# A two-layer MetaFormer on one core: four engine orders and the PSUM bank table replaced, column scans summed by GpSimd too, all stores last

## What is computed

```python
# conv block, on layer-normed x
feat = x @ in_w + in_b                      # 64 -> 3 * 64
inp, og, lam = silu(.), sigmoid(.), sigmoid(.)
inp_f = (1 - lam) (x) inp                   # 128 channels: every pair (d, e)
h_t = lam_t * h_{t-1} + inp_t               # along H and along W, forward and backward
state = fwd_h + rev_h + fwd_w + rev_w
out = layernorm(sum_d state * og) * gamma + beta
x = x + out @ out_w + out_b
# layer 0 experts: 16 of 128 hidden, top 2 of a softmax
x = x + sum_e gate[e] * ((silu(t @ w1[e]) * (t @ w2[e])) @ w3[e])
# layer 1 experts: 8 of 256 hidden, top 2
x = x + sum_e gate[e] * (gelu(t @ W1[e] + b1[e]) @ W2[e] + b2[e])
```

## Time and profile before

| | us |
|---|---|
| median of 3 runs | 237.87 (237.5 to 238.17) |
| the profiled execution, its own time | 238.65 |
| its span, first to last instruction | 236.4 |
| PE busy | 218.6 (92%) |
| DVE busy | 182.1 (77%) |
| ACT busy | 171.8 (73%) |
| POOL busy | 139.6 (59%) |
| mean granted TensorE clock | 0.993 of full |

### The profile page before, as it was taken

One profiled execution on the slowest core, in us unless ns is written; L12 is line 12 of the kernel. 1 busy time (PEld: TensorE's weight loads), 2 busy tenths in 40 slices (PEclk: granted clock), 3 DMA queues, 4 the chain that ended last, 5 costly groups with the idle time before them and its releaser, 6 DMA issues.

```text
span 236.4 us, 3790 instructions
## 1 busy us (share of the span) xinstructions
PE 218.6 (92%) x1078; PEld 139.6 (59%) x1078; DVE 182.1 (77%) x532; ACT 171.8 (73%) x407; POOL 139.6 (59%) x222
## 2 busy tenths in 40 slices
...
GB/s 104 12 185 194 176 2 3 0 6 175 209 152 6 182 174 0 10 209 146 27 223 114 0 3 0 5 135 42 0 3 177 4 1 0 3 193 11 142 82 22
DMA packets 19088, 18.51 MB, mean 78 GB/s; under 512 B 5606, under 2 KB 12924, under 8 KB 19068
## 3 DMA queue, kind: packets, MB, share of 16 engines
...
...
## 4 chain that ended last, share of the span: by engine, by line
PE 36%; DVE 28%; ACT 15%; issue 10%; POOL 9%; POOLq 0%; DVEq 0%; ACTq 0%
PE SPARE L1567 13%; PE SPARE L1427 9%; PE SPARE L1428 8%; DVE hidden L1338 5%; PE SPARE L1443 3%; ACT silu_h L1027 2%; ACT norm_e L901 2%; POOL rstd_e L754 2%; DVE SPARE L1248 2%; DVE gated L1281 2%; DVE fwd_w L1217 2%; DVE lam_rw L1227 2%; PE SPARE L1498 2%; POOL rstd_a L754 1%; DVE stats_e L1164 1%
## 5 line engine op out<-in xcount | busy, mean ns | idle before, releaser
L1427 PE MATMUL SPARE<-tok_z,up_hi 128*128 128x512 f32 x192 | 81.5, 424 | 2.6 <-DVE hidden L1338 2.1
L1428 PE MATMUL SPARE<-tok_z,up_lo 128*128 128x512 f32 x192 | 75.6, 394 | 0.0
L626 POOL TENSOR_TENSOR total<-total,weighted 128x512 f32<-128x512 f32 x39 | 50.2, 1286 | 32.0 <-DVE weighted L1362 19.6
L1567 PE MATMUL SPARE<-hidden,down 128*64 128x512 f32 x256 | 60.9, 603 | 1.1 <-DVE hidden L1338 0.8
L1027 ACT ACTIVATE silu_h<-SPARE 128x512 f32<-128x512 f32 x64 | 37.7, 599 | 22.0 <-PE SPARE L1428 19.7
L1427 PEld LDWEIGHTS SPARE<-tok_z,up_hi 128*128 128x128 f32 x192 | 36.1, 188 | 27.5 <-issue 13.0
L1338 DVE TENSOR_TENSOR hidden<-silu_h,SPARE 128x512 f32<-128x512 f32 x64 | 42.1, 678 | 9.5 <-ACT silu_h L1027 8.0
L1428 PEld LDWEIGHTS SPARE<-tok_z,up_lo 128*128 128x128 f32 x192 | 36.2, 189 | 5.8
L1567 PEld LDWEIGHTS SPARE<-hidden,down 128*64 128x64 f32 x256 | 16.1, 136 | 31.6 <-issue 25.4
L1034 ACT ACTIVATE hidden<-SPARE,expert_bias 128x512 f32<-128x512 f32 x32 | 21.9, 685 | 6.3 <-PE SPARE L1567 5.8
L1440 PE MATMUL SPARE<-ident 128*128 128x128 f32 x162 | 23.2, 302 | 3.0 <-POOL ident L726 1.9
...
## 6 DMA issues: line engine op xcount, KB each, us to landing
...
down<-in_L_ffn_w_dram SPq DMA_DIRECT2D x1, 512.0 KB, 10.8
...
```

Source lines behind the costliest of these rows:

```text
L626: nc_engine.tensor_tensor(t, t, weighted[:, q % WEIGHED_RING, :], ALU.add).then_inc(s_sum, 1)
L1427: nc.tensor.matmul(dst, hi, z, start=True, stop=False)
L1428: return nc.tensor.matmul(dst, lo, z, start=False, stop=True)
L1567: last = nc.tensor.matmul(spare("down", q)[k * D:(k + 1) * D, :], w, hidden[:, at, :], start=(j == 0), stop=(j == chunks - 1))
```

## The change

1. `SUM_WAYS` goes from `"w"` to `"wh"`: for chunks 2 to 8 POOL also sums the two column scans. Seven `sum_h` stages leave DVE's list and stand in POOL's; `rev_h` writes to `lam_rh` in SBUF and no longer to its PSUM bank; `sum_wh` reads `fwd_w` and `fwd_h`, both in SBUF; the next `lam_rh` waits for POOL's memset.
2. All four engine lists and the bank table are replaced. In the new ones the first expert products stand ahead of the projections of chunk 3 and of `heads2`, the scans of chunks 2 to 4 stand between `hid` stages, and the last `x_turn6` stands behind `down47`.
3. `BUSY_BEFORE` asks for 56 unneeded products where there were 81.
4. SP stores units 4 to 7 in a loop at the end; before, units 4 and 5 were stored behind the broadcasts of 6 and 7.

The diff, cut to its core:

```diff
--- before.py
+++ after.py
 
 SUM_BY_POOL = (2, 3, 4, 5, 6, 7, 8)
-SUM_WAYS = "w"
+SUM_WAYS = "wh"
 ADD_BY_VECTOR = (PAIRS[0] * GROUPS + PAIRS[1] * GROUPS - 1,)
 
     "PE": (
-        "a_turn0 a_turn1 b_turn0 p_f0 p_f1 p_i0 v_turn0 p_o0 p_i1 p_o1 products0 a_turn2 p_f2 p_i2 p_o2 a_turn3 "
-        "heads0 p_f3 p_i3 p_o3 heads1 e_turn0 e_turn1 heads2 up_a0 a_turn4 up_b0 logits0 up_a1 p_f4 p_i4 p_o4 "
-        "up_b1 up_a2 up_b2 up_a3 up_b3 g_turn0 heads3 up_a4 up_b4 up_a5 up_b5 up_a6 up_b6 up_a7 up_b7 up_a8 down0 "
-        "up_b8 e_turn2 up_a9 up_b9 up_a10 up_b10 up_a11 logits1 up_b11 up_a12 up_b12 up_a13 down2 heads4 up_b13 "
-        "up_a14 up_b14 up_a15 up_b15 up_a16 e_turn3 down4 up_b16 g_turn1 up_a17 up_b17 up_a18 up_b18 up_a19 "
...
-        "up_b93 down44 down45 up_a94 up_b94 up_a95 up_b95 down46 down47 x_turn7 "),
+        "a_turn0 a_turn1 b_turn0 p_f0 p_i0 v_turn0 p_o0 p_f1 p_i1 p_o1 products0 heads0 heads1 a_turn2 p_f2 p_i2 "
+        "p_o2 e_turn0 e_turn1 a_turn3 logits0 up_a0 up_b0 up_a1 up_b1 p_f3 p_i3 up_a2 up_b2 g_turn0 up_a3 up_b3 "
+        "up_a4 up_b4 up_a5 up_b5 p_o3 up_a6 up_b6 up_a7 up_b7 heads2 down0 up_a8 up_b8 a_turn4 up_a9 up_b9 up_a10 "
+        "p_f4 up_b10 p_i4 up_a11 down2 up_b11 up_a12 up_b12 up_a13 up_b13 heads3 up_a14 e_turn2 up_b14 up_a15 "
+        "logits1 up_b15 up_a16 down4 up_b16 up_a17 up_b17 g_turn1 up_a18 up_b18 up_a19 up_b19 up_a20 down6 up_b20 "
...
+        "up_a95 up_b95 down46 down47 x_turn6 x_turn7 "),
     "DVE": (
-        "a_stats0 a_stats1 a_parts0 a_parts1 in_w0 a_stats2 b_cols0 a_stats3 v_cols0 add_w0 fwd_w0 out_w0 rev_w0 "
-        "sum_w0 a_stats4 biases0 fwd_h0 rev_h0 add_w1 sum_h0 sum_wh0 fwd_h1 gate_o0 fwd_w1 rev_h1 rev_w1 sum_h1 "
-        "sum_w1 sum_wh1 add_w2 gate_o1 b_res0 fwd_h2 e_stats0 rev_h2 b_res1 sum_h2 fwd_w2 add_w3 rev_w2 e_parts0 "
-        "e_stats1 sum_wh2 in_w1 e_parts1 gate_o2 fwd_w3 fwd_h3 rev_w3 top0 rev_h3 hid0 b_res2 sum_h3 hid1 sum_wh3 "
...
-        "hid63 weigh30 weigh31 value7 weigh32 x_res3 add_w7 a_stats8 top5 fwd_w7 weigh33 fwd_h7 weigh34 rev_h7 "
-        "rev_w7 sum_h7 sum_wh7 gate_o7 value8 weigh35 add_w8 weigh36 x_res4 b_res7 e_stats7 fwd_h8 fwd_w8 rev_h8 "
-        "rev_w8 weigh37 sum_h8 weigh38 sum_wh8 gate_o8 top6 weigh39 b_res8 e_stats8 x_res5 weigh40 weigh41 top7 "
-        "weigh42 weigh43 x_res6 weigh44 weigh45 weigh46 weigh47 add47 x_res7 "),
+        "a_stats0 a_stats1 a_parts0 a_parts1 in_w0 a_stats2 b_cols0 a_stats3 v_cols0 add_w0 out_w0 fwd_w0 fwd_h0 "
+        "rev_w0 rev_h0 add_w1 sum_h0 sum_w0 biases0 sum_wh0 fwd_w1 fwd_h1 gate_o0 rev_w1 rev_h1 sum_w1 sum_h1 "
+        "sum_wh1 gate_o1 a_stats4 b_res0 e_stats0 b_res1 e_stats1 add_w2 e_parts0 e_parts1 fwd_h2 rev_h2 top0 "
+        "hid0 fwd_w2 hid1 rev_w2 add_w3 hid2 hid3 sum_wh2 hid4 gate_o2 hid5 fwd_h3 hid6 rev_h3 fwd_w3 weigh0 hid7 "
+        "rev_w3 hid8 b_res2 weigh1 e_stats2 hid9 hid10 sum_wh3 hid11 gate_o3 add_w4 weigh2 hid12 weigh3 hid13 "
+        "hid14 top1 hid15 b_res3 hid16 weigh4 hid17 weigh5 hid18 e_stats3 hid19 in_w1 weigh6 hid20 weigh7 hid21 "
+        "fwd_h4 hid22 hid23 x_res0 fwd_w4 a_stats5 hid24 weigh8 weigh9 rev_h4 hid25 hid26 rev_w4 hid27 weigh10 "
+        "hid28 weigh11 hid29 sum_wh4 gate_o4 top2 hid30 hid31 add_w5 weigh12 hid32 weigh13 hid33 b_res4 hid34 "
+        "hid35 fwd_w5 e_stats4 hid36 weigh14 hid37 weigh15 hid38 rev_w5 hid39 fwd_h5 weigh16 hid40 weigh17 hid41 "
+        "x_res1 rev_h5 hid42 a_stats6 hid43 sum_wh5 hid44 gate_o5 weigh18 weigh19 hid45 hid46 top3 hid47 weigh20 "
+        "hid48 weigh21 b_res5 hid49 e_stats5 hid50 add_w6 weigh22 weigh23 hid51 hid52 fwd_w6 hid53 hid54 x_res2 "
+        "a_stats7 weigh24 hid55 weigh25 hid56 fwd_h6 rev_w6 weigh26 hid57 weigh27 hid58 rev_h6 hid59 top4 sum_wh6 "
+        "hid60 gate_o6 weigh28 hid61 hid62 weigh29 hid63 value7 add_w7 weigh30 weigh31 b_res6 e_stats6 x_res3 "
+        "a_stats8 fwd_w7 rev_w7 weigh32 fwd_h7 rev_h7 top5 sum_wh7 gate_o7 weigh33 weigh34 value8 add_w8 b_res7 "
+        "weigh35 e_stats7 fwd_h8 weigh36 rev_h8 fwd_w8 rev_w8 sum_wh8 gate_o8 weigh37 weigh38 top6 b_res8 "
+        "e_stats8 weigh39 weigh40 weigh41 top7 x_res4 weigh42 weigh43 weigh44 weigh45 x_res5 weigh46 weigh47 "
+        "add47 x_res6 x_res7 "),
     "ACT": (
-        "in_hi0 b_wide0 a_z0 a_z1 v_wide0 t_f0 t_i0 lam_fw0 t_o0 lam_rw0 add_h0 a_norm2 gate_hi0 a_norm3 lam_fh0 "
-        "a_z2 lam_rh0 t_f1 t_i1 lam_fh1 t_o1 add_h1 lam_rh1 lam_fw1 round0 lam_rw1 a_z3 b_stats0 t_f2 t_i2 "
-        "lam_fh2 add_h2 lam_rh2 b_stats1 lam_rw2 lam_fw2 round1 t_o2 round2 t_f3 t_i3 in_hi1 lam_fh3 lam_fw3 "
...
+        "in_hi0 b_wide0 a_z0 a_z1 v_wide0 t_f0 t_i0 t_o0 lam_fw0 add_h0 lam_fh0 lam_rw0 lam_rh0 t_f1 t_i1 lam_fw1 "
+        "lam_fh1 add_h1 t_o1 lam_rw1 lam_rh1 a_norm2 round0 gate_hi0 b_stats0 a_norm3 b_stats1 a_z2 round1 t_f2 "
+        "t_i2 lam_fh2 lam_rh2 add_h2 lam_fw2 e_z0 round2 e_z1 round3 a_z3 lam_rw2 round4 act0 act1 t_f3 t_m0 act2 "
...
     "POOL": (
-        "a_rstd0 a_rstd1 a_rstd2 a_rstd3 a_parts2 gate_w0 a_rstd4 b_bias0 b_bias1 b_bias2 a_parts3 b_bias3 split0 "
-        "b_rstd0 b_rstd1 e_rstd0 split1 split2 sum_w2 e_rstd1 split3 a_parts4 b_bias4 b_rstd2 split4 split5 "
-        "sum_w3 split6 gates0 split7 b_rstd3 e_rstd2 e_parts2 sum_w4 add1 e_rstd3 e_parts3 add2 gates1 add3 "
...
-        "add35 b_rstd7 e_rstd7 e_parts7 sum_w8 add37 add38 gates6 b_rstd8 add39 e_rstd8 e_parts8 add41 gates7 "
-        "add42 add43 add45 add46 "),
+        "a_rstd0 a_rstd1 a_rstd2 b_bias0 a_rstd3 a_parts2 b_bias1 b_rstd0 split0 b_rstd1 e_rstd0 a_parts3 e_rstd1 "
+        "gate_w0 split1 a_rstd4 sum_h2 gates0 split2 b_bias2 sum_w2 split3 split4 split5 split6 split7 a_parts4 "
+        "b_rstd2 sum_h3 sum_w3 e_rstd2 b_bias3 add1 e_parts2 add2 b_rstd3 gates1 add3 add4 add5 e_rstd3 add6 add7 "
+        "b_bias4 e_parts3 a_rstd5 split8 sum_h4 a_parts5 sum_w4 b_bias5 add9 gates2 b_rstd4 add10 add11 add12 "
+        "add13 e_rstd4 add14 add15 e_parts4 sum_w5 sum_h5 a_rstd6 add17 split9 a_parts6 b_rstd5 gates3 add18 "
...
+        "sum_h7 sum_w7 gates5 add33 b_rstd7 add34 add35 e_rstd7 b_bias8 sum_h8 e_parts7 sum_w8 add37 b_rstd8 "
+        "gates6 e_rstd8 add38 add39 e_parts8 gates7 add41 add42 add43 add45 add46 "),
     "SP": (
-        "g_send0 g_back0 g_rest0 g_send1 g_back1 g_rest1 g_send2 g_back2 g_rest2 g_send3 g_back3 g_rest3 g_send4 "
-        "g_back4 g_rest4 g_send5 g_back5 g_rest5 g_send6 g_back6 g_rest6 g_send7 g_back7 g_rest7 "),
+        "g_send0 g_back0 g_rest0 load_w0 g_send1 g_back1 g_rest1 g_send2 g_back2 g_rest2 g_send3 g_back3 g_rest3 "
+        "g_send4 g_back4 g_rest4 g_send5 g_back5 g_rest5 g_send6 g_back6 g_rest6 g_send7 g_back7 g_rest7 "),
 }
...
 BUSY_BEFORE = (
-    "a_turn0:10 a_turn1:1 products0:9 p_f2:3 a_turn3:4 heads1:3 e_turn0:34 e_turn1:11 up_a1:3 up_b1:1 up_a5:2 ")
+    "a_turn0:10 a_turn1:1 products0:9 heads0:13 heads1:9 p_f2:3 e_turn0:9 up_b4:2 ")
 BUSY = {stages_of(name.split(":")[0])[0]: int(name.split(":")[1]) for name in BUSY_BEFORE.split()}
...
                 if u == 0:
                     sp.wait_ge(s_split, PAIRS[0])
                     load_up(2)
-                if u >= 2 and layer(u - 2):
-                    store_rows(u - 2)
-            for u in (UNITS - 2, UNITS - 1):
+            for u in range(UNITS - GROUPS, UNITS):
                 store_rows(u)
             sp.wait_ge(s_out, 16 * GROUPS)
 
```

25 lines of the change are left out of this document (12 added, 13 removed), and 115 rows, old and new, of tables (BANK_USES, ORDER).

## The result

| | before | after |
|---|---|---|
| median of the runs on this chip, us | 238.02 | 222.8 (222.26 to 223.4) |
| the profiled execution, us | 238.65 | 222.53 |
| its span, us | 236.4 | 220.7 |
| ratio of the runs | | 0.936 (0.933 to 0.940) |

The kernel is 15.2 us faster. The forecast was 232.3 us with a range down to 229.2, so the sign was right and the size was not: 5.6 us of gain were forecast, and 9.6 more came.

The account below looks back on a forecast made before the run. PE was taken to bound the kernel from 56 us on, DVE before that. 238.65 - 8.1 + 1.6 - 1.0 + 1.4 + 0.5 = 233.05 us, 232.3 in terms of the median; range 229.2 to 237.0 us.

Parts of the forecast that it names:

- the start: Ahead of the first expert products: ACT and DVE work moved away brings `up_a0` 8.1 us earlier, to about 31 us.
- the tail: After `add47`: `x_res6` lies ahead of `x_res7` and two stores leave close together, +0.5 us (0 to 1.2).
- the steady stage: Behind the first steps: PE's 4.6 us of idle stay; `sum_wh` and thinner DVE room cost +1.4 us (0 to 9).
- Holes up to the eighth step: From `up_a0` to `up_b7`: PE loses 4.7 us (3 to 6) where it lost 5.7, -1.0 us (-2.7 to +0.5).
- Work moved behind `up_a0`: On PE: chunk 3's projections and `heads2` come behind `up_a0`, `logits0` and `x_turn6` leave, +1.5 to +1.6 us.
- rival (a): All PE waits behind 56 us and the price of `sum_wh` go: 226 us at the far end, chance 0.10.
- `sum_wh`: On DVE: with two SBUF inputs it waits out POOL's running operation, 0.35 us each, seven times, 2.5 us.
- the stores: At the end on SP: moving the stores into the final loop costs nothing by itself.
- (b): PE's clock drops to half in stretches between 27 and 48 us: 236.1 to 237.0 us, chance 0.14.
- (c): From 31 to 145 us loaded DVE and PE spend the 5.6 us lead in small waits: 237.2 to 238.6, chance 0.08.
- (d): DVE stands at `sum_wh` for whole late POOL sums, 10.1 us instead of 1.4: 241.0 us, chance 0.12.

Follow-up runs that it names:

- the second profile of the kernel after: The changed kernel itself, nothing altered, run again on the same chip beside the run with split1 held back: 223.62 us, ratio 0.9373 to the kernel before.

## Why the prediction was wrong, step by step

The sum was 238.65 - 8.1 + 1.6 - 1.0 + 1.4 + 0.5 = 233.05 us; the profiled execution took 222.53. Of the 10.5 us between them 2.0 are the start, 7.6 lie between `up_a0` and `down47`, 0.5 are the tail and 0.4 lie outside the span. The step that failed most is the one on the steady stage: I added 1.4 us to it and left its idle time in place, and it became 4.5 us shorter.

**The start: right mechanism, too small.** `e_parts1` ends at 27.5 us, 10.0 us earlier, where I took 7.6. The stretch from the end of `gate_o1` to the end of `e_parts1` shrank from 13.5 to 7.6 us, by 5.9 (forecast 5.5). The mis-sized term is `gate_o1`: 4.1 us earlier and not 2.6. I had counted one wait of DVE, 0.97 us, and two DVE stages. The trace of before has two more waits in the same stretch:

```profile
11.25 0.69 DVE L1217 TENSOR_TENSOR_SCAN fwd_w<-lam_fw,SPARE 128x256 f32<-128x256 f32 x1 [0.82 <-ACT SPARE L992]
...
15.21 0.29 DVE L1147 COPY conv_bias<-SPARE 128x128 f32<-128x128 f32 x1 [0.78 <-PE SPARE L1443]
```

Of these three waits, 2.6 us, one of 0.35 us is left in the kernel after, so the two that I had not read (1.6 us, less those 0.35) are most of the missing 1.5 us. Putting only two of the three ACT stages back costs 1.9 us at the start, where DVE then waits 1.4 us for `lam_fh0`. I had also taken 0.5 us off for the chain through `heads1`, of which DVE shows one wait of 0.3 us.

**Holes up to the eighth step: the right limit, too small a term.** I laid the lists end to end, found 3 to 6 us of holes and took 4.7. In the forecast's own measure, `up_a0` to the end of `up_b7` is now 12.4 us, and its 38 products of 0.233 us and `g_turn0` are 8.9: 3.5 us lost where before it was 5.7. The term was -2.2 us and not -1.0, inside its bounds. The order of events was as drawn (`split2` ends at 35.0 us, `rev_w2` at 35.6, `split3` and `split4` together at 40.5). `up_a4` comes at 35.0 us and `up_a6` at 38.5, 2 to 3 us sooner than drawn, and 2.1 us of that are the start; PE waits for the split ahead of `up_a6` for 0.42 us.

**Work moved behind `up_a0`: counted right, and yet not seen in full.** I charged the projections of chunk 3 and `heads2` less `logits0` and `x_turn6` (+1.6), six records more. Without the unneeded products there are 833 records between `up_a0` and `down47` before and 839 after, so the count is right. PE's busy time without them rises by some 0.3 us only (an estimate: 182.4 - 1.9 against 181.4 - 0.6). Where the other 1.3 us went stays open.

**The steady stage: the sign was wrong, and this is the largest miss.** I charged +1.4 us for `sum_wh` and thin room on DVE, and left PE's 4.6 us of idle time there as it was. It fell to 1.5 us, and the length by 4.5. Thin room is real: DVE is busy for 71.0 of 74 us between 70 and 144 us:

```profile
70.00:144.00 74.00, 73.55 (x344) 45.91 (x343) 70.98 (x185) 56.97 (x133) 58.47 (x80) 1.00 0.37 77
```

PE idles 0.45 us in it. So here two nearly full engines hardly waited for each other; I read DVE's share as a cost and it was none. This was rival (a), to which I gave one chance in ten, and to which I held up just this argument. The result even lies beyond its far end, 226 us, because the start came out larger as well. The column sums, for which I charged, are worth 2.5 us there.

**`sum_wh`: the right place, another cause, too small.** Its mean is 1239 ns, 0.55 us above the 0.69, where I took 0.35. Two thirds of it is the turned read. On the path it is worth 0.9 to 1.2 us by the starts of `down47`, near the 1.4 charged; since the cause that I had named is only a third of it, that nearness is luck.

**The tail and the stores.** The tail costs 0.0 us and not 0.5, since `x_res6` fits beside `x_turn7`. The stores cost nothing, as forecast.

**The other rivals.** (b): the clock did not fall in the profiled run. Where it fell in other runs its price differed: 17 us at half went with 0.6 us at `down47` (without the unneeded products), 3.4 us went with 1.0 us (the second profile of the kernel after), and 6.8 us among the first steps of the old order went with 2.6 us more of PE's busy time and 3.3 us at `up_a8`. So (b) failed in this kernel, but its mechanism is real. (c): a lead is carried for the most part, 5.6 of 8.0 us. (d): POOL released `sum_wh` in time in all but one chunk, and the wait of 2.4 us there fell where DVE had room. That the old list with the sums on POOL came out at 240.9 us, where I had put 241.0 for (d), is a coincidence: DVE waited 4.6 us there and not 10.1, and where it cost nothing.

So the start (10.1 us) is shown, but what it is worth is not separable from what follows: with the old rest behind it the kernel is 3% slower, in part by a half clock, and with the new rest alone the time falls by 1.2%, with a start 6.7 us late. Where the 2.0 us of the steady gain that the order gives come from, chunk by chunk, stays open.
